# Graph layer on one NeuronCore: slot fill on the SyncE queue, node roots and residuals on GpSimd, a quarter of the node rows on VectorE

## The chip, the cores and the metric

One Trainium2 chip, one of its NeuronCores. The metric is the device time of one execution in microseconds (us). Times before: 1316.05, 1317.16 and 1323.12 us, median 1317.16.

## The reference

100,000 nodes with 160 features (64 scalars, 32 vectors of 3) and 25,000 edges sorted by `dst`. Cut to what matters:

```python
h = relu(layernorm(x))                          # per node, eps 1e-5
w = relu(edge_feature @ W_fc1) @ W_fc2          # 224 weights per edge
xs, xv = (s @ W_nl0)[dst], (v @ W_nl1)[dst]     # s, v: scalar and vector part of h
tp  = products of w, xs, xv and the edge's unit vector          # per edge, 480 values
agg = segment_sum(tp, src, N) / 32              # summed into the src node
out_s = agg_s @ W_out_s + s @ W_skip0
out_v = agg_v @ W_out_v + v @ W_skip1
x = x + [silu(out_s[:, :64]), sigmoid(out_s[:, 64:96]) * out_v]
```

## The kernel before

It is written engine by engine: each engine runs its own list of instructions in order, and semaphores tie them together. There are three stages.

**Opening.** Edges lie in 200 tiles of 125. A rank loop of 200 steps counts, for each edge, how many edges before it go to the same group of nodes: PE adds one-hots up (`count`, L1283), VectorE reads the result off (`tensor_tensor_reduce`, L648) and makes the next one-hot (L575). From the ranks VectorE makes `sidx` (L758), the row of the table `slots` in DRAM to which each edge's message goes. Meanwhile the table is filled with blank rows: 14 DMAs of 2744 KB each, issued by ScalarE (L1135). SyncE issues 20 small weight loads (L390) and the first edge features (L400). ScalarE, once its fills are issued, writes padding into the message ring `msg` (L1138), takes the square root for the unit vectors (L1141) and, when the weights are in, scales `fwd` (L1143). At step 30 of the rank loop PE multiplies `mirror` by `fwd` (L1346) and waits for that scaling. GpSimd gathers rows of x for the edges by indirect DMA (L495), `FIRST_GATHERS` = 132 tiles ahead of anything else.

**Edge stage.** 50 groups of 4 tiles. Per round PE makes the weights, rows and messages of a group, VectorE the products and the gathered rows' normalisation. On GpSimd four scatters (L505) write a finished group's messages to their slots, followed by as many gathers as the rule `due` (L526) asks for. GpSimd waits for the fill, for `sidx` and for the message (`e_fix`).

**Node stage.** 98 macro tiles of 1024 nodes (128 partitions, G = 8 rows each), in rounds. All engines go through `macros` (L341): 8 rounds written out, loops of 8, the rest written out. In round i:
- SyncE stores tile i-1 (`store_o`, L420) after its residual, loads the slots of tile i+3 (`load_m`) and x of tile i+7 (`load_x`, L407) into the place of the ring `xb` (8 places) that tile i-1 leaves.
- VectorE does `gate` (L984) for the two halves of a tile, `residual` (L998, adds x to the output), `hot_n` (L972, one-hots of the slots' local places), `stats_n` (L898, mean and variance of the rows of tile i+6). In one round of four (`u % U == 2`) it also turns the statistics of the next four tiles into n_rstd and n_bias: `spread`, `squares`, `variance`, `halve`, `seed`, three Newton steps, `shift_n` (L911 to L970). `n.ln` tells ScalarE.
- ScalarE normalises 8 rows of a tile, 4 in each half (`norm`, L1228), evacuates transposed rows with a relu (`evacuate`, L1237) and makes the gates' tanh and silu (L1242).
- PE transposes the normalised rows (`turn`), multiplies by the skip weights (`skip`), and adds the slots' messages (`add`).

GpSimd has nothing to do in the node stage.

## Time and profile before

| | |
|---|---|
| median of three runs | 1317.16 us |
| the profiled execution | 1322.71 us, its span 1320.8 us |
| PE, VectorE, ScalarE, GpSimd busy | 1114.8, 1026.3, 865.9, 442.2 us |
| opening | 0 to about 223 us |
| edge stage | to about 640 us |
| node stage | to the end |
| DMA moved | 271.10 MB |

The profile page gives an engine's busy time; what bounds a stage is read from the waits and from the chain of work that ended last. PE's busy time is modelled, since its matmuls overlap. Idle time counts only on the engine that the others wait for.

### The profile page before, as it was taken

How to read it: one execution, taken by the hardware profiler on the slowest of the kernel's cores; microseconds unless marked ns; L12 is line 12 of the kernel's file. 1: busy time of each engine (PE TensorE's matmuls, PEld its weight loads, DVE VectorE, ACT ScalarE, POOL GpSimd, SP SyncE). 2: the span in 40 equal slices, each digit the busy share in tenths (PEclk: the TensorE clock that was granted, in tenths of full speed). 3: DMA queues.
4: the chain of work that ended last, by engine and by line, in shares of the span. 5: the costliest groups of instructions: out<-in, count | busy, mean ns of one | idle time of the engine just before them, and what ended most of it. 6: DMA issues, size and time to landing. Idle time of an engine off the chain costs nothing.

```text
span 1320.8 us, 29100 instructions
## 1 busy us (share of the span) xinstructions
PE 1114.8 (84%) x8847; PEld 938.2 (71%) x8847; DVE 1026.3 (78%) x4002; ACT 865.9 (66%) x2070; POOL 442.2 (33%) x410
## 2 busy tenths in 40 slices
PE   5003998999999999989698999888998889988996
PEld 4002666888888888778577777777777777777775
DVE  8004998898888889776487888888888888888875
ACT  0003012787788778565677888788887888878884
POOL 6777710578787877777200000000000000000000
PEclk9556998999999999798699999999999999999998
DMA  9998200344544475444476677767777677666762
GB/s 358 406 406 308 66 23 9 91 132 133 130 130 135 129 244 176 122 114 123 128 256 241 246 265 255 252 230 262 257 259 259 222 264 256 250 252 239 261 213 108
DMA packets 108457, 271.10 MB, mean 205 GB/s; under 512 B 13573, under 2 KB 51751, under 8 KB 108364
## 3 DMA queue, kind: packets, MB, share of 16 engines
q1 hardware_dynamic: 76396, 194.15, 42.7%
q0 software_dynamic: 19200, 36.48, 9.4%
q10 hardware_dynamic: 12768, 39.34, 7.5%
q8 instruction: 45, 0.74, 0.2%
q14 instruction: 48, 0.39, 0.1%
HBM read 126.91 MB, written 143.01 MB: 204 GB/s over the span
## 4 chain that ended last, share of the span: by engine, by line
PE 35%; DVE 20%; issue 13%; POOL 13%; ACTq 8%; ACT 6%; DMA 2%; DVEq 0%; SPq 0%; POOLq 0%
POOL slots L505 9%; PE bank L1452 9%; ACTq L1135 8%; DVE n_stat L903 5%; DVE ob L994 4%; POOL xg L495 4%; PE bank L1465 4%; ACT nn L1233 4%; PE bank L1444 4%; PE bank L1284 3%; PE bank L1381 3%; PE bank L1456 2%; PE bank L1410 2%; DMA xb<-x 2%; PE bank L1316 2%
## 5 line engine op out<-in xcount | busy, mean ns | idle before, releaser
L1233 ACT ACTIVATE nn<-xb,n_bias,n_rstd 128x160 f32<-128x160 f32 x784 | 346.0, 526 | 87.8 <-DVE n_bias L634 87.8
L505 POOL DMA_INDIRECT slots<-msg,sidx x200 | 230.3, 1152 | 135.6 <-DVE sidx L758 71.4
L903 DVE BATCH_NORM_STATS2 n_stat<-xb 128x6 f32<-128x160 f32 x784 | 203.1, 314 | 11.9 <-DMA xb<-x 11.6
L994 DVE SCALAR_TENSOR_TENSOR ob<-sg,bank 128x128 f32<-128x128 f32 x588 | 132.7, 281 | 97.0 <-ACT ob L1248 95.8
L1452 PE MATMUL bank<-fwd,nt 128*128 128x160 f32 x784 | 146.5, 310 | 67.0 <-DVE ob L994 66.1
L1465 PE MATMUL bank<-mg,hot 64*128 64x192 f32 x1568 | 173.3, 340 | 9.2 <-DVE hot L979 9.2
L1452 PEld LDWEIGHTS bank<-fwd,nt 128*128 128x128 f32 x784 | 113.0, 191 | 81.4 <-issue 61.1
L495 POOL DMA_INDIRECT xg<-x,dst_i x136 | 148.6, 1093 | 44.1 <-issue 38.6
L1240 ACT ACTIVATE nt<-bank 128x640 f32<-128x640 f32 x196 | 137.2, 700 | 22.3 <-PE bank L1445 18.2
L1444 PE MATMUL bank<-ident,nn 128*128 128x128 f32 x784 | 147.0, 311 | 2.6 <-ACT nn L1233 2.6
L1001 DVE TENSOR_TENSOR ob<-ob,xb 128x1280 f32<-128x1280 f32 x98 | 146.0, 1490 | 2.6
L1444 PEld LDWEIGHTS bank<-ident,nn 128*128 128x128 f32 x784 | 109.1, 207 | 47.3 <-issue 46.2
L648 DVE CUSTOM_DVE_ANT_0 rank_junk<-bin_hot,bank 125x196 bf16<-125x196 f16 x200 | 70.6, 353 | 91.8 <-PE bank L1284 91.8
L1452 PE MATMUL bank<-rev,nt 128*128 128x160 f32 x784 | 140.3, 302 | 0.0
L1465 PEld LDWEIGHTS bank<-mg,hot 64*128 64x128 f32 x1568 | 125.6, 190 | 9.4 <-DVE hot L979 9.4
L1452 PEld LDWEIGHTS bank<-rev,nt 128*128 128x128 f32 x784 | 118.8, 193 | 0.0
L1189 ACT ACTIVATE tpt<-bank 128x375 f32<-128x375 f32 x200 | 96.6, 483 | 33.6 <-PE bank L1381 33.3
L1381 PE MATMUL bank<-ident,tp 125*128 125x125 f32 x600 | 107.7, 290 | 8.0 <-DVE tp L829 7.4
L1381 PEld LDWEIGHTS bank<-ident,tp 125*128 125x128 f32 x600 | 70.9, 150 | 43.3 <-issue 28.8
L1456 PE MATMUL bank<-fwd,nt 64*128 64x64 f32 x392 | 85.5, 299 | 0.0
L1456 PE MATMUL bank<-rev,nt 64*128 64x64 f32 x392 | 85.5, 298 | 0.0
L979 DVE TENSOR_TENSOR hot<-iota_local,mg 128x256 f32<-128x256 f32 x196 | 75.9, 419 | 11.5 <-DMA mg<-slots 11.5
(181 smaller groups left out, 2399.7 us busy)
## 6 DMA issues: line engine op xcount, KB each, us to landing
xb<-x SPq DMA_DIRECT2D x97, 640.0 KB, 5.1
out_dram<-ob SPq DMA_DIRECT2D x97, 640.0 KB, 3.3
slots<-blank ACTq DMA_DIRECT2D x14, 2744.0 KB
mg<-slots SPq DMA_DIRECT2D x98, 392.0 KB, 4.0
messages<-msg SPq DMA_DIRECT2D x50, 382.8 KB
ef<-edge_feat_t SPq DMA_DIRECT2D x50, 125.0 KB
slots<-msg,sidx POOLq DMA_INDIRECT x200, 4.3
xg<-x,dst_i POOLq DMA_INDIRECT x136, 6.8
```

The costliest lines, as they stand in the source:

```text
L495: pool.indirect_dma_start(rows_of(g)[:, t, :], None, x[:, :], bass.IndirectOffsetOnAxis(ap=dst_i[:, m:m + 1], axis=0)).then_inc(e_x[g % XS ...
L505: pool.indirect_dma_start(slots[:, :], bass.IndirectOffsetOnAxis(ap=sidx[:, m:m + 1], axis=0), msg[:, c, t, 0:MW], None).then_inc(e_sc[c], 16)
L903: done = dve.bn_stats(n_stat[:, u // U, u % U * G + g, :], xb[:, u, g, :])
L994: last = dve.scalar_tensor_tensor(out=o[:, :, S + V * j:S + V * j + V], in0=sg[:, h, :, :], scalar=1.0, in1=z[:, :, part], op0=ALU.add, op ...
L1001: dve.tensor_tensor(o, o, xb[:, u, :, :], ALU.add).then_inc(n.res, 1)
L1233: last = act.activation(nn[:, u % 2, h, spread_of(g % 4)], xb[:, u, g, order_of(g % 4)], ACT.Relu, bias=n_bias[:, u // U, c:c + 1], scale= ...
L1240: act.activation(nt[:, h, :], q_t[h], ACT.Relu).then_inc(n.ht, 1)
L1381: last = pe.transpose(p_tt[:, i * ET:(i + 1) * ET], tp[:, c, t, TURN[i]:TURN[i] + P], idt)
L1444: pe.transpose(q_t[h][:, t * P:(t + 1) * P], nn[:, u % 2, h, main_of(t)], ident[:])
L1452: pe.matmul(z[:, t, 0:F], nt[:, h, t * P:(t + 1) * P], sides[t // 2][:, skip_cols], start=(t % 2 == 0), stop=False, skip_group_check=True)
L1456: pe.matmul(z[:, 2 * j:2 * j + 2, F:Z], nt[part, h, 4 * P:5 * P], sides[j][part, skip_z_cols], start=False, stop=every, skip_group_check=True)
L1465: last = pe.matmul(q_z[h][:, t, 0:Z], hot[slots, u % 2, pair, :], mg[slots, u % U, pair, 0:Z], start=False, stop=True, skip_group_check=True)
```

## The change

**Opening.** The 14 fills go to SyncE, behind its first four edge loads; the weight loads go to ScalarE, ahead of all else there; the square root comes before the padding. VectorE blanks `blank` after the weight tiles. PE multiplies `mirror` by `fwd` at step 60 instead of 30. `FIRST_GATHERS` is 104 instead of 132, and `due` is smaller.

```diff
-    FIRST_GATHERS = 132
+    FIRST_GATHERS = 104
...
-                sp.wait_ge(s_clr, 1)
-                for to, of in weight_loads:
-                    sp.dma_start(to, of).then_inc(s_w, 16)
...
                 for q in range(ER):
                     load_f(q)
+                sp.wait_ge(s_blank, 2)
+                for k in range(NM // FILL):
+                    rows = slots[k * (FILL * BPM * P):(k + 1) * (FILL * BPM * P), :]
+                    sp.dma_start(rows.rearrange("(b p k) c -> p b (k c)", p=P, k=BPM),
+                                 blank[:, 0:BPM * MW].unsqueeze(1).to_broadcast((P, FILL, BPM * MW))).then_inc(s_fill, 16)
...
-                    due = min(NT, max(FIRST_GATHERS + 3 * (p + 1) // 2, GE * (p + 12)))
+                    due = min(NT, max(FIRST_GATHERS + 2 * (p + 1), GE * (p + 10)))
...
             def _(act):
+                act.wait_ge(s_clr, 1)
+                for to, of in weight_loads:
+                    act.dma_start(to, of).then_inc(s_w, 16)
+                act.wait_ge(s_tab, 1)
+                act.activation(vec_r[:], vec_d2[:], ACT.Sqrt).then_inc(s_sqrt, 1)
                 act.wait_ge(s_blank, 2)
-                for k in range(NM // FILL):
...
-                    if t == 30:
+                    if t == 60:
                         pe.wait_ge(s_fwd, 1)
```

**Node stage.** From tile 4 on GpSimd makes the roots with a power of -0.5, per tile (`root`), from sums that it makes for four tiles at once (`spread`); it also does the residual. VectorE keeps the root work of tiles 0 to 3. VectorE normalises row 3 of each half by a multiply-add without the relu, which `evacuate` applies anyway; ScalarE does the other three. PE's transposes wait for both. The statistics of a tile are made in two halves, before and after a gate. ScalarE and VectorE now wait for the shifts of one tile, not of four.

```diff
+                def nodes(n):
+                    def spread(j, w):
...
+                        pool.wait_ge(n.stats, min(j + U, NM) if isinstance(j, int) else j + U)
+                        pool.tensor_tensor(sums[:, 0, :], stat[:, :, 1], stat[:, :, 4], ALU.subtract)
+                        pool.tensor_tensor(sums[:, 1, :], stat[:, :, 2], stat[:, :, 5], ALU.add).then_inc(n.chain, 1)
+                        pool.tensor_tensor(sums[:, 2, :], stat[:, :, 1], stat[:, :, 4], ALU.add).then_inc(n.spread, U)
+                        pool.wait_ge(n.chain, base + 1)
+                        pool.tensor_tensor(sums[:, 3, :], sums[:, 0, :], sums[:, 0, :], ALU.mult)
+                        pool.tensor_scalar(sums[:, 1, :], sums[:, 1, :], 1.0 / F, EPS, ALU.mult, ALU.add).then_inc(n.chain, 1)
+                        pool.wait_ge(n.chain, base + 2)
...
+                        pool.tensor_scalar(sums[:, 3, :], sums[:, 3, :], 0.25, None, ALU.mult).then_inc(n.chain, 1)
+                        pool.wait_ge(n.chain, base + 3)
+                        pool.tensor_tensor(sums[:, 4, :], sums[:, 3, :], sums[:, 1, :], ALU.add).then_inc(n.chain, 1)
+                    def root(v, w):
...
+                        pool.tensor_tensor(n_rstd[:, b, cols], n_sum[:, b, 4, cols], neg_half[:], ALU.pow
+                                           ).then_inc(n.chain, 1)
+                        pool.tensor_scalar(n_sum[:, b, 2, cols], n_sum[:, b, 2, cols], -0.5, None, ALU.mult
+                                           ).then_inc(n.half, 1)
+                        pool.wait_ge(n.chain, base + 5 + k)
+                        pool.wait_ge(n.half, v - U + 1)
+                        pool.tensor_tensor(n_bias[:, b, cols], n_sum[:, b, 2, cols], n_rstd[:, b, cols], ALU.mult
+                                           ).then_inc(n.ln, 1)
+                    def residual(i, u):
+                        pool.wait_ge(n.mul, 2 * i + 2)
+                        o = ob[:, u % U, :, :]
+                        pool.tensor_tensor(o, o, xb[:, u, :, :], ALU.add).then_inc(n.res, 1)
+                    def round_n(i, u):
+                        v, w = i + 2, (u + 2) % XU
+                        if macro_exists(v) and macro_exists(i - 2):
+                            if w % U == 0:
+                                spread(v, w)
+                            root(v, w)
+                        if macro_exists(i - 1):
+                            residual(i - 1, (u + 7) % XU)
...
+                    def norm(i, u, h):
+                        dve.wait_ge(n.ln, i + 1)
+                        wait(dve, n.t, 2 * (i - 2) + h + 1)
+                        g = 4 * h + 3
+                        c = u % U * G + g
+                        dve.tensor_scalar(nn[:, u % 2, h, spread_of(3)], xb[:, u, g, order_of(3)],
+                                          n_rstd[:, u // U, c:c + 1], n_bias[:, u // U, c:c + 1],
+                                          ALU.mult, ALU.add).then_inc(n.norm_d, 1)
...
                         if macro_exists(i - 1):
                             gate(i - 1, before, 1)
...
+                        if macro_exists(i + 1):
+                            norm(i + 1, after, 1)
                         if macro_exists(i + 1) and not every:
                             hot_n(i + 1, after, 0)
                             hot_n(i + 1, after, 1)
...
+                        if measure:
+                            stats_n(s, v, 0, 4)
                         gate(i, u, 0)
...
+                        if macro_exists(i + 2):
+                            norm(i + 2, (u + 2) % XU, 0)
+                        if measure:
+                            stats_n(s, v, 4, 8)
...
-                        for g in range(4 * h, 4 * h + 4):
+                        for g in range(4 * h, 4 * h + 3):
...
                         pe.wait_ge(n.norm, 2 * i + h + 1)
+                        pe.wait_ge(n.norm_d, 2 * i + h + 1)
```

VectorE in two node rounds without root work, before (gates in banks 2 and 3 are the halves 0 and 1 of a tile):

```order
L994 SCALAR_TENSOR_TENSOR ob<-sg,bank3 128x4x32 x3
L1001 TENSOR_TENSOR ob<-ob,xb 128x1280
L979 TENSOR_TENSOR hot<-iota_local,mg 128x256 x2
L903 BN_STATS n_stat<-xb 128x6 x8
L994 SCALAR_TENSOR_TENSOR ob<-sg,bank2 128x4x32 x3
L994 SCALAR_TENSOR_TENSOR ob<-sg,bank3 128x4x32 x3
```

And now, in every round:

```order
L1066 SCALAR_TENSOR_TENSOR ob<-sg,bank3 128x4x32 x3
L1052 TENSOR_SCALAR nn<-xb,n_rstd,n_bias 128x160
L1042 TENSOR_TENSOR hot<-iota_local,mg 128x256 x2
L966 BN_STATS n_stat<-xb 128x6 x4
L1066 SCALAR_TENSOR_TENSOR ob<-sg,bank2 128x4x32 x3
L1052 TENSOR_SCALAR nn<-xb,n_rstd,n_bias 128x160
L966 BN_STATS n_stat<-xb 128x6 x4
```

The residual over 1280 columns is gone from VectorE, two multiply-adds over 160 columns have come, and the second half of the statistics stands behind a gate.

GpSimd, which had nothing behind its last scatter, now, from there on: a residual, the spread and root of tile 4, then a root and a residual for each tile (a spread every fourth):

```order
L513 DMA slots<-msg,sidx 50776x196 x36
L575 TENSOR_TENSOR ob<-ob,xb 128x1280
L545 TENSOR_TENSOR n_sum<-n_stat 128x32
L546 TENSOR_TENSOR n_sum<-n_stat 128x32
L547 TENSOR_TENSOR n_sum<-n_stat 128x32
L549 TENSOR_TENSOR n_sum<-n_sum 128x32
L550 TENSOR_SCALAR n_sum<-n_sum 128x32
L553 TENSOR_SCALAR n_sum<-n_sum 128x32
L555 TENSOR_TENSOR n_sum<-n_sum 128x32
L563 TENSOR_TENSOR n_rstd<-n_sum,neg_half 128x8
L565 TENSOR_SCALAR n_sum<-n_sum 128x8
L569 TENSOR_TENSOR n_bias<-n_sum,n_rstd 128x8
```

All node work of GpSimd stands behind its 200 scatters. Behind the spread and root comes the next residual (L575).

SyncE at the start of the program, now; the fills stand where the weight loads were, one place later:

```order
L394 DMA vec<-edge_vec 125x600
L403 DMA ef<-edge_feat_t 128x250 x4
L411 DMA slots<-blank 128x7x784 x14
L403 DMA ef<-edge_feat_t 128x250 x4
L398 DMA messages<-msg 125x4x196
```

The first edge loads have moved ahead of the fills, and the loads for round 4 and after stand behind all 14 of them.

## Rows read from the trace of the kernel before

**Rows 1.** The page's first line.
```profile
span 1320.8 us, 29100 instructions
```

**Rows 2.** The waits of the whole span: engine, line, released by, total us, times, longest.
```profile
ACT L1138 <- issue: 106.2, 1, 106.2
...
PE bank L1346 <- ACT fwd L1143: 89.0, 1, 89.0
ACT nn L1233 <- DVE n_bias L634: 87.8, 24, 4.2
POOL slots L505 <- DVE sidx L758: 71.4, 1, 71.4
PE bank L1452 <- DVE ob L994: 66.1, 47, 2.0
...
DVE n_stat L903 <- DMA xb<-x: 11.6, 24, 1.0
```

**Rows 3.** Timeline of GpSimd: start us, us, instruction, idle before and its releaser.
```profile
170.97 0.97 POOL L495 DMA_INDIRECT xb<-x,dst_i  x1 [0.30 <-issue]
243.29 1.00 POOL L505 DMA_INDIRECT slots<-msg,sidx  x1 [71.36 <-DVE sidx L758]
...
302.62 1.93 POOL L505 DMA_INDIRECT slots<-msg,sidx  x1 [0.30 <-issue]
...
638.87 0.97 POOL L505 DMA_INDIRECT slots<-msg,sidx  x1 [0.30 <-issue]
```

**Rows 4.** Busy us by stretch: PE, PEld, DVE, ACT, POOL; clock, DMA share, GB/s.
```profile
250.00:300.00 50.00, 50.00 (x413) 43.89 (x412) 45.82 (x174) 39.40 (x88) 39.99 (x33) 1.00 0.49 132
...
800.00:900.00 100.00, 88.36 (x729) 74.60 (x729) 84.87 (x319) 80.29 (x205) 0.00 (x0) 1.00 0.70 250
```

**Rows 5.** Groups of GpSimd, 260 to 500 us: busy us, mean ns, idle before.
```profile
L505 POOL DMA_INDIRECT slots<-msg,sidx x115 | 142.2, 1236 | 35.0 <-issue 31.7 <-DVE msg L845 3.4
L495 POOL DMA_INDIRECT xg<-x,dst_i x43 | 51.3, 1193 | 13.1 <-issue 11.0 <-DVE msg L845 2.1
```

**Rows 6.** The chain that ended last, in order of time, node stage.
```profile
777.74 1.32 PE bank L1452 x8
...
1240.42 1.32 PE bank L1452 x8
```

**Rows 7.** Timeline of SyncE's queue, first and last weight loads of 20.
```profile
3.34 4.82 SPq L390 DMA_DIRECT2D wfc<-W_fc  x4
...
31.15 1.53 SPq L390 DMA_DIRECT2D fwd<-W_nl  x1
```

**Rows 8.** DMA queues, 38 to 42 us: packets, MB, share (q1 is SyncE's).
```profile
q1 hardware_dynamic: 285, 0.26, 19.0%
```

**Rows 9.** Timeline of ScalarE, the scaling of `fwd`.
```profile
115.86 0.29 ACT L1143 ACTIVATE fwd<-fwd 128x128 f32<-128x128 f32 x1
```

**Rows 10.** Timeline of VectorE, one operation of two scalars over 200 columns.
```profile
4.50 0.27 DVE L565 TENSOR_SCALAR hi<-src_i 125x200 int32<-125x200 int32 x1 [0.66 <-DMA dst_i<-dst]
```

**Rows 11.** Timeline of VectorE and of SyncE's queue in a node round.
```profile
912.74 0.68 DVE L994 SCALAR_TENSOR_TENSOR ob<-sg,bank 128x128 f32<-128x128 f32 x3
...
916.56 1.49 DVE L1001 TENSOR_TENSOR ob<-ob,xb 128x1280 f32<-128x1280 f32 x1
...
919.40 0.80 SPq L409 DMA_DIRECT2D xb<-x  x1
...
924.50 1.91 DVE L903 BATCH_NORM_STATS2 n_stat<-xb 128x6 f32<-128x160 f32 x8 [0.45 <-DMA xb<-x]
```

**Rows 12.** Groups of GpSimd, 0 to 180 us: its work other than DMA.
```profile
L511 POOL TENSOR_SCALAR_AFFINE_SELECT ident<-ident 128x128 f32<-128x128 f32 x1 | 0.4, 410 | 0.0
...
L513 POOL TENSOR_SCALAR_AFFINE_SELECT mirror<-mirror 128x128 f32<-128x128 f32 x1 | 0.3, 282 | 0.0
...
L1543 POOL MEMSET const-float32-0.0<- 128x1 f32 x1 | 0.1, 98 | 0.3 <-issue 0.3
```

**Rows 13.** Timeline of VectorE, a product with both inputs in SBUF, edge stage.
```profile
302.61 0.42 DVE L823 TENSOR_TENSOR cr_b<-w4xv,hat 125x256 f32<-125x256 f32 x1
```

More of the change, by code:

```diff
@@ L254, in __init__ @@
                 self.root = sem(f"{name}_root")
+                self.stats = sem(f"{name}_stats")
+                self.spread = sem(f"{name}_spread")
+                self.chain = sem(f"{name}_chain")
+                self.half = sem(f"{name}_half")
+                self.norm_d = sem(f"{name}_norm_d")
                 self.ln = sem(f"{name}_ln")
@@ L529, in _ @@
                     made = max(made, due)
+                def nodes(n):
+                    def spread(j, w):
+                        b, base = w // U, 2 * (j - U)
+                        stat, sums = n_stat[:, b, :, :], n_sum[:, b, :, :]
+                        pool.wait_ge(n.stats, min(j + U, NM) if isinstance(j, int) else j + U)
[6 more added lines that the diff above has]
+                        pool.wait_ge(n.chain, base + 2)
+                        pool.sem_inc(s_held, 1)
+                        pool.tensor_scalar(sums[:, 3, :], sums[:, 3, :], 0.25, None, ALU.mult).then_inc(n.chain, 1)
+                        pool.wait_ge(n.chain, base + 3)
+                        pool.tensor_tensor(sums[:, 4, :], sums[:, 3, :], sums[:, 1, :], ALU.add).then_inc(n.chain, 1)
+                    def root(v, w):
+                        k, b = w % U, w // U
+                        base, cols = 2 * (v - k - U), slice(w % U * G, w % U * G + G)
+                        pool.wait_ge(n.chain, base + 4 + k)
+                        wait(pool, n.norm, 2 * (v - XU) + 2)
+                        wait(pool, n.norm_d, 2 * (v - XU) + 2)
+                        pool.tensor_tensor(n_rstd[:, b, cols], n_sum[:, b, 4, cols], neg_half[:], ALU.pow
[18 more added lines that the diff above has]
+                            residual(i - 1, (u + 7) % XU)
+                    macros(pool, round_n)
+                    residual(NM - 1, (NM - 1) % XU)
@@ L531, in _ @@
+                pool.wait_ge(s_half, 1)
+                nodes(main)
                 pool.wait_ge(b_fin, 1)
@@ L901, in stats_n @@
                             dve.wait_ge(n.x[u], earlier(i, u, XU, 16) + 16)
+                            if u % U == 0:
+                                wait(dve, n.spread, i - XU)
                         for g in range(first, last):
                             done = dve.bn_stats(n_stat[:, u // U, u % U * G + g, :], xb[:, u, g, :])
-                        if last == G and (u % U == U - 1 or isinstance(i, int) and i == NM - 1):
-                            done.then_inc(n.root, 1)
+                        if last == G:
+                            done.then_inc(n.stats, 1)
                     def level(i, u):
@@ L914, in spread @@
                         stat, sums = n_stat[:, b, :, :], n_sum[:, b, :, :]
-                        dve.wait_ge(n.root, base + 1)
+                        dve.wait_ge(n.stats, U)
                         dve.tensor_tensor(sums[:, 0, :], stat[:, :, 1], stat[:, :, 4], ALU.subtract)
@@ L922, in squares @@
                         sums = n_sum[:, b, :, :]
-                        dve.wait_ge(n.root, base + 2)
+                        dve.wait_ge(n.root, base + 1)
                         dve.tensor_tensor(sums[:, 3, :], sums[:, 0, :], sums[:, 0, :], ALU.mult)
@@ L936, in halve @@
                         b, base = u // U, level(i, u)
-                        dve.wait_ge(n.root, base + 4)
+                        dve.wait_ge(n.root, base + 3)
                         dve.tensor_scalar(n_seed[:, b, :], n_sum[:, b, 4, :].bitcast(I32), 1, None,
@@ L943, in seed @@
                         wait(dve, n.norm, 2 * (i - U))
-                        dve.wait_ge(n.root, base + 5)
+                        dve.wait_ge(n.root, base + 4)
                         dve.tensor_scalar(n_rstd[:, b, :].bitcast(I32), n_seed[:, b, :], -1.0, SEED, ALU.mult,
@@ L950, in root_a @@
                         y = n_rstd[:, b, :]
-                        dve.wait_ge(n.root, base + 7)
+                        dve.wait_ge(n.root, base + 6)
                         dve.tensor_tensor(n_step[:, b, 0, :], y, y, ALU.mult).then_inc(n.root, 1)
@@ L962, in root_c @@
                         y = n_rstd[:, b, :]
-                        dve.wait_ge(n.root, base + 9)
+                        dve.wait_ge(n.root, base + 8)
                         dve.scalar_tensor_tensor(out=y, in0=n_step[:, b, 1, :], scalar=1.5, in1=y,
@@ L968, in shift_n @@
                         b, base = u // U, level(i, u)
-                        dve.wait_ge(n.root, base + 16)
+                        dve.wait_ge(n.root, base + 15)
                         shift(n_bias[:, b, :], n_sum[:, b, :, :], n_rstd[:, b, :]).then_inc(n.ln, U)
@@ L996, in gate @@
                         last.then_inc(n.mul, 1)
-                    def residual(i, u):
-                        dve.wait_ge(n.mul, 2 * i + 2)
-                        o = ob[:, u % U, :, :]
-                        dve.tensor_tensor(o, o, xb[:, u, :, :], ALU.add).then_inc(n.res, 1)
                     def places(i):
```

66 lines of the change are left out of this document (11 added, 55 removed).

## The prediction

> **What bounds the kernel now.** I read the page first, then the waits, then timelines of the three stages, then the chain. The span is 1320.8 us [rows 1].
>
> The opening. The waits [rows 2] name one cause under three heads: ScalarE's first activation waits 106.2 us for its own queue, which is issuing the 14 fills of the slot table; PE waits 89.0 us at step 30 of the rank loop for `fwd`, which ScalarE scales only after that, and VectorE waits with it; GpSimd waits 71.4 us for `sidx`, which the rank loop ends in. GpSimd's last opening gather starts at 170.97, its first scatter at 243.29 [rows 3].
>
> The edge stage. From 250 on PE is 50.00 busy of 50 [rows 4], but GpSimd is full too: between 260 and 500 its 115 scatters and 43 gathers take 193.5 us of issue and 48.1 us of gaps [rows 5], the whole 240 us, and only 5.5 us of the gaps wait for a message of VectorE. So it is behind the other engines, and its last scatter, begun at 638.87 [rows 3], opens the node stage. That is 396.5 us for 268 indirect DMAs, 1.48 us each.
>
> The node stage. The chain passes the same instruction every fourth macro tile at 777.74 and, 17 such steps on, at 1240.42 [rows 6]: 27.2 us for four, 6.8 for one. PE is busy 88.36 of 100 us [rows 4], so without waits four would take about 24.0. The rest are waits around the one round in four in which VectorE also does the root: PE for the gate 66.1 us, ScalarE for the shifts 87.8 us; loads of `xb` cost VectorE only 11.6 us [rows 2].
>
> **Part 1, fill and loads change queues.** ScalarE now issues the 20 weight loads first. On SyncE they went out from 3.34 to 32.7, 1.5 us each beside the same fill [rows 7]. By 38 to 42 that queue moves packets of 0.9 KB, edge rows that were queued behind the weights [rows 8], so the weights are through by then. What stands between the queue's end and `fwd` on ScalarE, the square root and the padding of `msg`, takes 115.9 - 106.2 = 10 us [rows 9, 2], so `fwd` is ready near 43. PE asks for it at step 60. It stood at step 30 at 116 - 89 = 27 us, which bounds 30 steps from above, and the 170 steps after the wait run until the `sidx` of rows 3 at 243, so at least 0.5 us each: step 60 falls between 42 and 54, and the wait is gone or a few us. I leave 3 us for that and for slower steps beside GpSimd's gathers. On SyncE only four edge loads stand ahead of the fill, and the next thing behind it is an edge load for round 4, after the fill is out; the fill's issue ended at 106 us [rows 2] and shifts by a few us, so it stays well ahead of the first scatter. Rank loop and first scatter move by 89 - 3 = 86 us, to 157.
>
> GpSimd does not get all of that. It issues 104 gathers first instead of 132, at 1.25 us (0.95 and a gap of 0.30 [rows 5, 3]): done at 172 - 35 = 137, idle for 20. Then 296 indirect DMAs are left, 28 more than before. At 1.48 us they take 438 us: last scatter at 595 instead of 640. **Gain 45 us.** The mean between 260 and 500, 1.52 us, would give 607 and 33 us; all 86 us would come only if GpSimd were no limit, which its full issue contradicts, but its DMAs are quicker when PE and VectorE stall. I keep 25 to 60.
>
> **Part 2, node rounds.** ScalarE loses two of eight activations of 526 ns a round; VectorE loses the residual of 1.49 us and all root work and gains two multiply-adds over 160 columns, 0.24 us each (200 columns took 0.27 [rows 10]). The waits for shifts go: roots are now made by GpSimd ahead of time. What is late next is the load of `xb`. SyncE may load x(i+7) only after the residual of tile i-1, which frees the buffer, and VectorE's statistics of x(i+7) come two rounds later than that residual. One residual ends at 918.05, its x load, the third on the queue, is issued at 919.40, and the statistics that need it start at 924.50 after a wait [rows 11]: 6.45 us. Only 0.45 us of it is waited for now. A longer residual lengthens exactly this ring.
>
> The new ring over two rounds: 6.45 for the load; half the statistics 0.90 (half of 1.91); gate 0.60 (0.68, the next begins 0.60 after its start); multiply-add 0.20; second half 0.95: 9.1. Then either the gate of the other half and a handover, 0.85, and the residual r; or, once in four rounds, GpSimd's spread and root s, which wait for those statistics and stand ahead of the residual on its queue, and then r. Four rounds: 2 x 9.1 + 0.85 + 2r + s = 19.05 + 2r + s.
>
> The trace shows no such work on GpSimd. For r the nearest row is its own masked copy of 128 columns, 282 ns [rows 12]: ten times that, 2.8 us, which I take. Ends: VectorE's 1.49 us for the same residual, and the slower copy, 410 ns, times ten, 4.1 us. For s, ten small instructions and five waits on itself: taken 0.28 x 10 + 5 x 0.15 = 3.5; ends 1.0 (ten of its 98 ns fills, no handover) and 4.1 + 1.5 = 5.6 (the slow copy, gaps of 0.30). Sum 19.05 + 5.6 + 3.5 = 28.2 against 27.2. **Loss** 1.0 x 24.5 = **25 us**, with ends of 24.0 (PE's floor), a gain of 78, and 32.9, a loss of 140. If the ring is as computed, VectorE's and ScalarE's relief is worth nothing.
>
> Edits that cost nothing: the start of the residual on GpSimd in the last tile (1.3 us, in the rounding), the -0.5 fill, the extra semaphores.
>
> **Sum.** The profiled execution took 1322.7 us with its launch: 1322.7 - 45 + 25 = 1302.7. It lay 5.5 us above the median of the three runs, 1317.2, so I give 1298.
>
> **Rivals.**
> (a) GpSimd and VectorE stop each other. In the edge stage a scatter takes 1.93 us instead of 0.97 when it falls into VectorE's back-to-back products (302.61 and 302.62 [rows 13, 3]), while those products keep their 0.42 us, as long as the 256-column one-hots of the node stage. If each residual loses that 1.0 us to the two one-hots and the multiply-add that VectorE sends right behind the gate that releases it, r is 3.8, four rounds take 30.2, and the loss is 3.0 x 24.5 = 74 us: 1317 - 45 + 74 = 1346, slower. It decides from r = 3.2 on, where the whole gain of 45 is eaten up. For it: the order of VectorE's round. Against: here they are three instructions of 0.9 us in all, against a run of eight there. By the Trainium skill ("SBUF — State Buffer", Who interferes with whom), a VectorE instruction with two SBUF inputs and a GpSimd one that reads SBUF exclude each other for a whole instruction, whichever starts first. By that rule VectorE's one-hots could wait out a whole residual, too, but they stand ahead of a wait for the x load that is as long, so only the residual's own delay counts; the stretched scatter agrees with a lock, the unchanged products do not show it in the other direction.
> (b) GpSimd adds nearly as fast as VectorE: r = 1.5 to 2.0, s = 2.5, four rounds in 24.6 to 25.6, a gain of 40 to 64: 1208 to 1232. For it: if 98 of the copy's 282 ns are a fixed start, as in the one-column fill, ten times the rest and one start make 1.9 us. Against: the copy reads one input, the residual two. By the Trainium skill ("GPSIMD Engine Reference", Performance versus the Vector engine) a two-input add there takes 1.96 times VectorE's time; an estimate by it is 2.9 us for this residual, and 1304 where the sum has 1298.
> (c) The weights land only with the fill, so that `fwd` waits for 112 us as before and the rank loop still stands from step 60: first scatter at 224, 296 DMAs then end at 662, 22 us later than now: 1317 + 22 + 25 = 1364. Rows 8 speak against it.
> (d) The change does not do what it says, because GpSimd reaches the node work late: it comes after the last scatter on its queue. Node rounds cannot start before that scatter anyway.
>
> **Chances.** Forecast (both parts as computed, r near 2.8) 0.52; (a) 0.19; (b) 0.19; (c) 0.05; the rest, in both directions, 0.05. The forecast's own range, from a gain of 25 to 60 us in part 1 and r within 0.4 of 2.8 (20 us), is 1263 to 1338. For 8 in 10 I reach over most of (a) and into (b): 1230 to 1352, which leaves out the better half of (b), (c) and the top of (a). A measurement here can tell about 0.5%, 6.6 us, from no change. Faster by more: three quarters of the forecast, (b) and 0.02 of the rest, 0.60. Within: an eighth of the forecast and the mild fifth of (a), 0.11. Slower: what is left of these, (c) and 0.03 of the rest, 0.29.
>
> **What would show it.** Right: PE's wait at the mirror matmul gone; first scatter near 157 after a GpSimd idle time near 20; last scatter near 595; in the node stage, VectorE waiting for `xb<-x` by 1 to 3 us in most rounds, chain through GpSimd's residual and that load, four tiles in 28. Wrong: residuals under 2 us, or x loads not waited for; a first scatter after 200; VectorE's one-hots stretched past 1 us with nothing waiting for x.

## The result, and the profile after

| | before | after |
|---|---|---|
| time, median | 1319.8 us (4 runs, 1316.1 to 1323.1) | 1352.0 us (4 runs, 1347.5 to 1356.7) |
| profiled execution: time, span | 1322.7, 1320.8 us [rows 1] | 1348.3, 1346.5 us |
| after / before | | 1.0245, 95% interval 1.0189 to 1.0301 |
| four macro tiles, node stage | 27.2 us [rows 6] | 30.7 us |

The change makes the kernel 2.5% slower; 1298 us was predicted, faster. One execution of run 5 below took 2505 us, nearly twice its other three, and stands in none of its figures. Line numbers of the kernel after are its own: the residual on GpSimd is L575, the power L563, VectorE's multiply-add L1052, its one-hots L1042, its gate L1066, its statistics L966.

**The opening went as computed.** GpSimd's timeline, to be held against [rows 3]:

```profile
137.45 1.04 POOL L503 DMA_INDIRECT xb<-x,dst_i  x1 [0.30 <-issue]
148.80 1.01 POOL L513 DMA_INDIRECT slots<-msg,sidx  x1 [10.31 <-DVE sidx L819]
...
586.44 0.97 POOL L513 DMA_INDIRECT slots<-msg,sidx  x1 [0.30 <-issue]
```

The first scatter starts at 148.8 after 10.3 us of idle time (predicted: 157 and 20), the last at 586.4 instead of 638.9 (predicted: 595). So the node stage starts 52 us earlier, and all of that and 32 us more is lost later. The wait at the mirror matmul is gone: ScalarE scales `fwd` at 37.11.

```profile
37.11 0.31 ACT L1174 ACTIVATE fwd<-fwd 128x128 f32<-128x128 f32 x1
```

**The node stage waits for x.** The waits of the whole span, against [rows 2]:

```profile
DVE n_stat L966 <- DMA xb<-x: 173.5, 74, 5.4
...
POOL ob L575 <- DVE ob L1066: 96.3, 49, 14.0
PE bank L1484 <- DVE ob L1066: 94.1, 52, 4.7
POOL n_sum L545 <- DVE n_stat L966: 75.8, 22, 4.0
...
ACT nn L1264 <- POOL n_bias L569: 56.0, 43, 1.7
...
DVE ob L1066 <- ACT ob L1279: 41.8, 39, 2.9
```

VectorE's wait for the loads of x grew from 11.6 to 173.5 us, while ScalarE's for the shifts fell from 87.8 to 56.0. The windows (columns as in [rows 4]) show that no engine is full in this stage, and that PE's granted clock, 1.00 there before, is 0.89:

```profile
800.00:900.00 100.00, 83.83 (x623) 70.45 (x621) 71.48 (x233) 62.46 (x153) 74.15 (x74) 0.89 0.64 228
```

**The ring, row by row.** The ring is the circle residual, load of x into the place that it frees, statistics of that x, gate, next residual. One period of four tiles in the timelines of GpSimd, VectorE and SyncE's queue:

```profile
917.74 2.91 POOL L575 TENSOR_TENSOR ob<-ob,xb 128x1280 f32<-128x1280 f32 x1
...
922.01 0.76 SPq L417 DMA_DIRECT2D xb<-x  x1
...
927.09 1.00 DVE L966 BATCH_NORM_STATS2 n_stat<-xb 128x6 f32<-128x160 f32 x4 [3.90 <-DMA xb<-x]
...
929.78 0.66 DVE L1066 SCALAR_TENSOR_TENSOR ob<-sg,bank 128x128 f32<-128x128 f32 x3
...
930.52 3.63 POOL L575 TENSOR_TENSOR ob<-ob,xb 128x1280 f32<-128x1280 f32 x1 [1.96 <-DVE ob L1066]
...
935.52 0.77 SPq L417 DMA_DIRECT2D xb<-x  x1
...
940.94 1.01 DVE L966 BATCH_NORM_STATS2 n_stat<-xb 128x6 f32<-128x160 f32 x4 [0.22 <-DMA xb<-x]
...
943.80 0.29 POOL L545 TENSOR_TENSOR n_sum<-n_stat 128x32 f32<-128x32 f32 x1 [3.69 <-DVE n_stat L966]
...
946.01 1.67 POOL L563 TENSOR_TENSOR n_rstd<-n_sum,neg_half 128x8 f32<-128x8 f32 x1
...
948.14 2.91 POOL L575 TENSOR_TENSOR ob<-ob,xb 128x1280 f32<-128x1280 f32 x1
```

Read downwards, each row starts when the one above it lets it: a residual of 2.91; 6.44 us until the statistics of the x that it lets in; 3.43 through statistics, gate, multiply-add and second gate to the next residual; that residual, 3.63; 6.79 to the next statistics; 2.86 to the spread; spread and root 4.34, of which the power alone is 1.67; and the residual again. The sum is 30.40 us. Over nine such periods the mean is 30.70, by the residuals ahead of the spread, in GpSimd's timeline:

```profile
906.91 2.96 POOL L575 TENSOR_TENSOR ob<-ob,xb 128x1280 f32<-128x1280 f32 x1 [1.50 <-DVE ob L1066]
...
1183.21 2.96 POOL L575 TENSOR_TENSOR ob<-ob,xb 128x1280 f32<-128x1280 f32 x1 [1.73 <-DVE ob L1066]
```

This is the ring that the prediction described, and it closes; its terms were too small. In the period shown no step of the ring waits for PE or ScalarE. The ring is read from the waits: the profile's own chain stays on GpSimd's queue here and passes no load of x between 626 and 1259 us.

**Each engine holds the other up.** The groups of VectorE and GpSimd in the whole span (busy us, mean ns of one):

```profile
L1042 DVE TENSOR_TENSOR hot<-iota_local,mg 128x256 f32<-128x256 f32 x196 | 134.8, 727 | 10.6 <-DMA mg<-slots 10.6
L1052 DVE TENSOR_SCALAR nn<-xb,n_rstd,n_bias 128x160 f32<-128x160 f32 x196 | 125.5, 641 | 0.8 <-POOL n_bias L569 0.4
...
L575 POOL TENSOR_TENSOR ob<-ob,xb 128x1280 f32<-128x1280 f32 x98 | 303.9, 3101 | 96.3 <-DVE ob L1066 96.3
L563 POOL TENSOR_TENSOR n_rstd<-n_sum,neg_half 128x8 f32<-128x8 f32 x94 | 156.6, 1666 | 3.3 <-POOL n_sum L555 2.2
```

The one-hots took 419 ns each before, as the groups of that kernel have it:

```profile
L979 DVE TENSOR_TENSOR hot<-iota_local,mg 128x256 f32<-128x256 f32 x196 | 75.9, 419 | 11.5 <-DMA mg<-slots 11.5
```

The means of the one-hots and the multiply-adds after hide two kinds each, as VectorE's timeline shows beside two residuals (906.91 to 909.87, and 930.52 to 934.15 above):

```profile
907.02 3.47 DVE L1042 TENSOR_TENSOR hot<-iota_local,mg 128x256 f32<-128x256 f32 x2
...
917.95 2.79 DVE L1052 TENSOR_SCALAR nn<-xb,n_rstd,n_bias 128x160 f32<-128x160 f32 x1
...
930.63 0.75 DVE L1042 TENSOR_TENSOR hot<-iota_local,mg 128x256 f32<-128x256 f32 x2
```

At 907.02 the pair of one-hots ends only after the residual; at 930.63 it takes its usual 0.75 us and the residual 3.63 instead of 2.91. The multiply-add of 917.95, 0.36 us elsewhere, lasts until the residual of 917.74 ends.

### The profile page after: what moved, and what is told of

Its sections match the earlier page's. It is cut to its first block, busy times and chain, and to the rows that moved or that the text cites. A ratio compares the mean times of both kernels' runs of the same rounds, so it can differ in the third digit from the quotient of the medians.

```text
span 1346.5 us, 29745 instructions
## 1 busy us (share of the span) xinstructions
PE 1158.7 (86%) x8847; PEld 972.3 (72%) x8847; DVE 1001.3 (74%) x3669; ACT 805.8 (60%) x1873; POOL 1005.6 (75%) x958
## 4 chain that ended last, share of the span: by engine, by line
issue 32%; POOL 29%; PE 26%; DVE 7%; DMA 3%; POOLq 1%; SPq 0%; ACT 0%; DVEq 0%
POOL n_rstd L563 9%; POOL ob L575 6%; POOL slots L513 6%; POOL xg L503 4%; PE bank L1412 4%; PE bank L1315 3%; PE bank L1441 3%; PE bank L1347 2%; PE bank L1429 2%; DVE bin_hot L636 2%; PE bank L1425 2%; PE bank L1484 2%; PE bank L1427 2%; DMA xb<-x 2%; DVE rank_junk L709 2%
## 5 line engine op out<-in xcount | busy, mean ns | idle before, releaser
L575 POOL TENSOR_TENSOR ob<-ob,xb 128x1280 f32<-128x1280 f32 x98 | 303.9, 3101 | 96.3 <-DVE ob L1066 96.3
L966 DVE BATCH_NORM_STATS2 n_stat<-xb 128x6 f32<-128x160 f32 x784 | 196.0, 311 | 173.5 <-DMA xb<-x 173.5
L1264 ACT ACTIVATE nn<-xb,n_bias,n_rstd 128x160 f32<-128x160 f32 x588 | 264.0, 521 | 56.2 <-POOL n_bias L569 56.0
L1484 PE MATMUL bank<-fwd,nt 128*128 128x160 f32 x784 | 156.6, 325 | 94.7 <-DVE ob L1066 94.1
L1484 PEld LDWEIGHTS bank<-fwd,nt 128*128 128x128 f32 x784 | 122.5, 205 | 111.5 <-issue 70.0
L1497 PE MATMUL bank<-mg,hot 64*128 64x192 f32 x1568 | 185.7, 359 | 10.9 <-DVE hot L1042 10.9
L1476 PE MATMUL bank<-ident,nn 128*128 128x128 f32 x784 | 153.4, 321 | 10.4 <-DVE nn L1052 9.8
L1066 DVE SCALAR_TENSOR_TENSOR ob<-sg,bank 128x128 f32<-128x128 f32 x588 | 130.9, 277 | 41.9 <-ACT ob L1279 41.8
L563 POOL TENSOR_TENSOR n_rstd<-n_sum,neg_half 128x8 f32<-128x8 f32 x94 | 156.6, 1666 | 3.3 <-POOL n_sum L555 2.2
L1278 ACT ACTIVATE sg<-bank 128x128 f32<-128x128 f32 x196 | 53.0, 271 | 172.5 <-PE bank L1497 145.6
L1497 PEld LDWEIGHTS bank<-mg,hot 64*128 64x128 f32 x1568 | 135.0, 202 | 11.0 <-DVE hot L1042 11.0
L1042 DVE TENSOR_TENSOR hot<-iota_local,mg 128x256 f32<-128x256 f32 x196 | 134.8, 727 | 10.6 <-DMA mg<-slots 10.6
L1052 DVE TENSOR_SCALAR nn<-xb,n_rstd,n_bias 128x160 f32<-128x160 f32 x196 | 125.5, 641 | 0.8 <-POOL n_bias L569 0.4
## 6 DMA issues: line engine op xcount, KB each, us to landing
slots<-blank SPq DMA_DIRECT2D x14, 2744.0 KB, 30.7
```

The source lines that it names most:

```text
L563: pool.tensor_tensor(n_rstd[:, b, cols], n_sum[:, b, 4, cols], neg_half[:], ALU.pow).then_inc(n.chain, 1)
L575: pool.tensor_tensor(o, o, xb[:, u, :, :], ALU.add).then_inc(n.res, 1)
L966: done = dve.bn_stats(n_stat[:, u // U, u % U * G + g, :], xb[:, u, g, :])
L1042: made = dve.tensor_tensor(hot[:, u % 2, bins, :], iota_local[:].unsqueeze(1).to_broadcast((P, 2, P)), mg[:, m, bins, LOCAL:LOCAL + 1].to_ ...
L1264: last = act.activation(nn[:, u % 2, h, spread_of(g % 4)], xb[:, u, g, order_of(g % 4)], ACT.Relu, bias=n_bias[:, u // U, c:c + 1], scale= ...
L1476: pe.transpose(q_t[h][:, t * P:(t + 1) * P], nn[:, u % 2, h, main_of(t)], ident[:])
```

## The experiments

Two theories stood against each other. **Ring theory**: the load of x waits for the residual, so whatever GpSimd does between the statistics and the end of the residual lengthens the node stage. **Lock theory**: GpSimd's residual and VectorE's one-hots and multiply-adds stop each other, and that is what costs. Each run has 4 executions (run 3 has 10), the kernel before 7 or 13 on the same chip (medians 1321.1, 1320.2 and 1323.2 us in the order of the three groups: 1 to 4, 5 to 8, 9 to 12). Ratios are to that kernel; differences to the change are to its 1352.0 us, and a few us between runs of different groups say nothing.

### 1. The opening alone

The kernel before with the first half of the change: fill on SyncE, weights on ScalarE, fewer gathers ahead. Its moves of fill and weights are those of the change; the rest of its edit:

```diff
-    FIRST_GATHERS = 132
+    FIRST_GATHERS = 104
...
-                    due = min(NT, max(FIRST_GATHERS + 3 * (p + 1) // 2, GE * (p + 12)))
+                    due = min(NT, max(FIRST_GATHERS + 2 * (p + 1), GE * (p + 10)))
...
-                    if t == 30:
+                    if t == 60:
```

> The kernel before with the opening of the change alone (fill on SyncE, weight loads on ScalarE, step 60, 104 first gathers), its node stage as before. If the two parts add up, this keeps what the profile of after shows for the opening, a last scatter at 586 instead of 639 us, and loses nothing in the node stage at 27.2 us for four tiles: about 1320 - 52 = 1267 us. If the opening's gain were given back in the node stage by other means (the fill's queue, the clock), it would stay above 1300.

Measured 1272.9 us, ratio 0.9646 (0.961 to 0.968). Part 1 gains 48 us by itself, so part 2 loses 79 from there, not 25.

### 2. The residual back on VectorE

The first line stood in GpSimd's round, the second comes in VectorE's.

```diff
-                            residual(i - 1, (u + 7) % XU)
...
                             gate(i - 1, before, 1)
+                            residual(i - 1, before)
```

> The changed kernel with the residual back on VectorE, right behind the gate that ends a tile; roots stay on GpSimd, one row in four on VectorE. Ring theory (the load of x waits for the residual; residual, power and spread on GpSimd make the ring long): the ring has neither a GpSimd residual nor the roots in it, 6.45 + 3.25 + 1.5 = 11.2 us for two tiles, so PE's 24 to 25 us for four sets the pace: 1352 - 6 x 24.5 = about 1205 to 1215 us. Lock theory (GpSimd's two-input work stops VectorE's two-input and one-source work wherever they meet): the power of 1.67 us still stops VectorE once a tile, now also its residual, VectorE has 5.6 + up to 1.7 us of work a tile: 27 to 29 us for four, 1260 to 1310 us.

Measured 1227.1 us, ratio 0.9289 (0.925 to 0.933): 125 us less than the change, 12 us above the ring theory's figure and 33 us below the lock theory's. VectorE's wait for the loads of x falls from 173.5 to 4.5 us, and PE is busy 95 of 100 us at a clock of 1.00, as that kernel's windows show:

```profile
900.00:1000.00 100.00, 95.25 (x790) 80.85 (x787) 91.48 (x300) 76.24 (x190) 47.35 (x77) 1.00 0.75 269
```

### 3 and 4. A root without the power; the one-hots ahead of the gate

In run 3 the root is a product: the roots themselves are left out, so the normalised values are others. In run 4 VectorE's multiply-add and one-hots come ahead of the gate that releases the residual.

```diff
-                        pool.tensor_tensor(n_rstd[:, b, cols], n_sum[:, b, 4, cols], neg_half[:], ALU.pow
+                        pool.tensor_tensor(n_rstd[:, b, cols], n_sum[:, b, 4, cols], neg_half[:], ALU.mult
```

> The changed kernel with a product in place of the power of -0.5 on GpSimd, so the roots are left out and the rows are scaled wrongly; the work is otherwise the same. A product over 8 columns should take 0.2 us instead of 1.67. Ring theory: the ring holds the power once in four tiles, so four tiles take 1.45 us less: 1352 - 36 = 1316 us. If GpSimd's total time were the bound (its busy share is 75%), all four powers would count: 1352 - 142 = 1210. If neither, no change.

Measured 1325.4 us, ratio 1.0043 (1.001 to 1.008): 27 us less than the change, 9 us short of what the ring theory gave. The product in its groups:

```profile
L563 POOL TENSOR_TENSOR n_rstd<-n_sum,neg_half 128x8 f32<-128x8 f32 x94 | 19.1, 203 | 3.3 <-POOL n_sum L555 2.2
```

It took 203 ns against 1666, and 1.46 us once in four tiles is 36 us; GpSimd was not full (56 to 60 of 100 us busy between 700 and 1200 us). The residuals, 3280 ns in the mean, were held longer than in the change, which can be the 9 us; that is not shown. The power stands in the ring.

```diff
-                        if macro_exists(i - 1):
-                            gate(i - 1, before, 1)
                         if macro_exists(i + 1):
                             norm(i + 1, after, 1)
...
+                        if macro_exists(i - 1):
+                            gate(i - 1, before, 1)
```

> The changed kernel with VectorE's multiply-add and one-hots of a round moved ahead of the gate that releases GpSimd's residual; nothing else. Lock theory: they no longer run into the residual, so one-hots fall from a mean of 0.73 us to 0.42 and the multiply-add from 0.64 to under 0.5; what the measured 30.7 us for four tiles has above the ring's 29.3 goes: 1.4 x 24.5 = 34 us, about 1318 us. Ring theory without a lock: these instructions stand in the wait for x anyway, 1345 to 1355 us.

Measured 1363.1 us, ratio 1.0318 (1.027 to 1.037). The lock theory expected a gain and missed; the ring theory's 1345 to 1355 was 8 us too low. Groups of that kernel:

```profile
L1042 DVE TENSOR_TENSOR hot<-iota_local,mg 128x256 f32<-128x256 f32 x196 | 74.0, 418 | 20.6 <-DMA mg<-slots 10.6 <-PE bank L1497 9.7
...
L575 POOL TENSOR_TENSOR ob<-ob,xb 128x1280 f32<-128x1280 f32 x98 | 284.9, 2907 | 123.8 <-DVE ob L1066 123.8
```

The one-hots are down to 418 ns, the residuals to 2.91 us each, and still it takes 11 us longer: the 61 us of one-hot time that were saved had been spent where VectorE then waited for x anyway (those waits grow from 173.5 to 242.5 us), and the two instructions now stand in the ring, ahead of the gate: from statistics to residual 4.38 us (906.49 to 910.87 in that kernel's timeline), against 3.43. The multiply-adds of the other half round stayed held (635 ns), so this run does not speak about them.

### 5 and 6. All normalising on ScalarE

```diff
-                        for g in range(4 * h, 4 * h + 3):
+                        for g in range(4 * h, 4 * h + 4):
```

VectorE's `norm` and its waits go. Run 5 does this to the change, run 6 to run 2, so that only the roots and shifts of part 2 stay on GpSimd.

> The change, with all four rows of a half tile normalised on ScalarE again; the two multiply-adds of VectorE per tile are gone, the residual and the roots stay on GpSimd. In the change these multiply-adds take 641 ns each in the mean (125.5 us for 196) and as little as 349 ns where nothing stretches them: 57 us are stretch, and each stretched one stands ahead of the second half of the statistics, whose buffer had landed. Ring theory alone (no stop between the engines): the ring loses two multiply-adds of 0.36 us in four tiles, 0.72 x 24.5 = 18 us, to about 1334. Lock theory (GpSimd's residual holds the multiply-add up, and that delay lies in the ring): the 57 us go as well, to about 1277. Either way ScalarE gets 0.9 us more a tile, 62 of 100 us busy now, some 76 then, which should not bind.

Measured 1347.9 us, ratio 1.0239 (1.017 to 1.031): 4 us less than the change, which is no difference, so both theories missed. Its lines of the waits show where the 57 us of held multiply-adds may have gone:

```profile
DVE n_stat L965 <- DMA xb<-x: 227.2, 68, 6.9
...
DVE ob L1065 <- ACT ob L1271: 86.3, 73, 3.2
```

VectorE's waits for ScalarE, whose fourth row stands ahead of the activations that the gate needs, doubled to 86.3 us, and those for x grew by 54. That the fourth row is the cause was not tested.

> The change with the residual and all normalising where they were before (VectorE right behind the gate; ScalarE), so that of part 2 only the roots and shifts are GpSimd's. Against the run with the residual on VectorE and one row of four on VectorE (1227.1 us), it tells what the multiply-add is worth: VectorE is 91.5 of 100 us busy there and PE 95. Either theory: if VectorE's load is what is left, 0.7 us a tile less for it gives 0 to 20 us, 1207 to 1227; if ScalarE, which waits 64.9 us for shifts there and would get 0.9 us a tile more, becomes the late one, 1235 to 1255. Against the opening alone (1272.9 us) it tells what moving only the roots gives.

Measured 1211.6 us, ratio 0.9173 (0.914 to 0.921). Beside VectorE's own residual the multiply-adds cost 15 us. Run 6 against run 1 is the worth of moving the roots: 61 us, together with the halved statistics and the waits for the shifts of one tile, which run 6 keeps.

### 7. The load of x first

The wait for the residual moves out of `store_o` to the head of SyncE's round.

```diff
                         if macro_exists(i - 1):
-                            store_o(i - 1, (u + 7) % XU)
-                        if macro_exists(i + U - 1) and not every:
-                            load_m(i + U - 1, (u + U - 1) % XU)
+                            sp.wait_ge(n.res, i)
                         if isinstance(i, int) and i + 7 == NM - 1:
                             load_last((u + 7) % XU)
                         elif macro_exists(i + 7) and macro_exists(i - 1):
                             load_x(i + 7, (u + 7) % XU)
+                        if macro_exists(i - 1):
+                            store_o(i - 1, (u + 7) % XU)
+                        if macro_exists(i + U - 1) and not every:
+                            load_m(i + U - 1, (u + U - 1) % XU)
```

> The change, with SyncE's three DMAs of a round in another order: the load of x(i+7) first, then the store of tile i-1, then the slot rows. No engine's work changes. In the change the load is issued 1.36 us after the residual that frees its buffer ends, behind the store and the slot rows; here some 0.25. Ring theory: two such loads stand in the ring of four tiles, so it loses 2 x 1.1 = 2.2 us, 54 us in all, to about 1298. Lock theory (what costs is that GpSimd's residual and VectorE's one-hots and multiply-adds stop each other): nothing of that changes, 1345 to 1355.

Measured 1296.2 us, ratio 0.9828 (0.978 to 0.987), where the ring gave 1298. The load now leaves 0.19 us after its residual's end, as one period of that kernel's timeline has it:

```profile
892.43 2.90 POOL L577 TENSOR_TENSOR ob<-ob,xb 128x1280 f32<-128x1280 f32 x1
...
895.52 0.33 SPq L417 DMA_DIRECT2D xb<-x  x1
...
900.76 1.01 DVE L968 BATCH_NORM_STATS2 n_stat<-xb 128x6 f32<-128x160 f32 x4 [2.88 <-DMA xb<-x]
...
904.20 3.63 POOL L577 TENSOR_TENSOR ob<-ob,xb 128x1280 f32<-128x1280 f32 x1 [0.96 <-DVE ob L1068]
...
913.12 1.01 DVE L968 BATCH_NORM_STATS2 n_stat<-xb 128x6 f32<-128x160 f32 x4 [0.72 <-DMA xb<-x]
...
916.26 0.28 POOL L547 TENSOR_TENSOR n_sum<-n_stat 128x32 f32<-128x32 f32 x1 [1.10 <-DVE n_stat L968]
...
920.60 2.91 POOL L577 TENSOR_TENSOR ob<-ob,xb 128x1280 f32<-128x1280 f32 x1
```

The period is 28.17 us instead of 30.40. From a residual's end to the statistics it has 5.43 and 5.29 us instead of 6.44 and 6.79; the residuals, 2.90 and 3.63, and spread and root, 4.34, are as they were, the hold included. No engine's work changed, yet 56 us are gone. In the mean its residuals are held longer than in the change (3212 ns), its one-hots less (520 ns, 41 us in all); but run 4 freed the one-hots wholly and gained nothing. This run decides between the theories.

### 8. Eight more gathers first

```diff
-    FIRST_GATHERS = 104
+    FIRST_GATHERS = 112
```

> The run with the residual on VectorE (1227.1 us), with 112 instead of 104 gathers ahead of the first scatter. In the change GpSimd stands idle 10.3 us ahead of that scatter; eight more gathers of 1.25 us fill it, and the last scatter should come 8 to 10 us earlier: 1217 to 1219. If the first scatter comes later by as much, or gathers that follow wait for buffers, 1227.

Measured 1219.1 us, ratio 0.9221 (0.917 to 0.927): this is run 2 with that edit, and 8 us less than run 2.

### 9. The residual ahead of the root

```diff
+                        if macro_exists(i - 1):
+                            residual(i - 1, (u + 7) % XU)
                         if macro_exists(v) and macro_exists(i - 2):
                             if w % U == 0:
                                 spread(v, w)
                             root(v, w)
-                        if macro_exists(i - 1):
-                            residual(i - 1, (u + 7) % XU)
```

> The change, with GpSimd's round in another order: the residual of tile i-1 ahead of the spread and the root for tile i+2. The same work. In the change the residual that is queued behind the spread starts 4.0 us after its gate is through (gate through at 913.76, residual at 917.74). Ring theory, by the ring alone: 4.0 to 4.4 us of four tiles go, 98 to 108 us, to 1244 to 1254. If the shifts then become the late thing (spread and root end one residual of 2.9 us later, and ScalarE, which waits 1.7 us for them once in four tiles now, waits some 4.6): at most 2.9 of the 4.4 us come back, about 1315. Lock theory: VectorE's one-hots now meet a residual in every round, 1350 or more.

Measured 1443.1 us, ratio 1.0908 (1.087 to 1.095): both figures of the ring theory missed, and the lock theory's "1350 or more" covers it. VectorE waits no more for x (0.0 us), and another ring has closed, one round long. GpSimd, ScalarE and VectorE in that kernel's timeline:

```profile
907.73 2.96 POOL L575 TENSOR_TENSOR ob<-ob,xb 128x1280 f32<-128x1280 f32 x1 [2.67 <-DVE ob L1066]
...
910.66 1.84 POOL L563 TENSOR_TENSOR n_rstd<-n_sum,neg_half 128x8 f32<-128x8 f32 x1
...
913.11 1.35 ACT L1264 ACTIVATE nn<-xb,n_bias,n_rstd 128x160 f32<-128x160 f32 x3 [3.39 <-POOL n_bias L569]
...
914.51 0.36 ACT L1279 ACTIVATE ob<-bank 128x256 f32<-128x256 f32 x1
...
914.98 0.68 DVE L1066 SCALAR_TENSOR_TENSOR ob<-sg,bank 128x128 f32<-128x128 f32 x3 [0.60 <-ACT ob L1279]
...
915.74 2.95 POOL L575 TENSOR_TENSOR ob<-ob,xb 128x1280 f32<-128x1280 f32 x1 [2.67 <-DVE ob L1066]
```

The root waits behind the residual, ScalarE's normalising for the root, the activations for the gate behind that on ScalarE's queue, and the next residual for the gate: 8.01 us a round, and some 10.4 in the one with the spread. I had counted one late shift in four tiles; there is one in every tile. The one-hots are held in every round (1757 ns in the mean), but every row above is released by the one before it, and none of them is a held one; only the root is 0.17 us longer than in the change. Three rounds of 8.01 and one of 10.4 make 34.4 us for four tiles, 91 us more than the change over the node stage, which is what was measured.

### 10. Half the residual

Four of the eight row groups get no residual in this run.

```diff
-                        o = ob[:, u % U, :, :]
-                        pool.tensor_tensor(o, o, xb[:, u, :, :], ALU.add).then_inc(n.res, 1)
+                        o = ob[:, u % U, 0:G // 2, :]
+                        pool.tensor_tensor(o, o, xb[:, u, 0:G // 2, :], ALU.add).then_inc(n.res, 1)
```

> The change, with GpSimd's residual over four of the eight row groups only; the other half of the residual is left out. Ring theory: two residuals stand in the ring of four tiles, 2.91 and 3.63 us, and each loses half: 3.2 us, 78 us in all, to about 1274. If GpSimd's own time set the pace, all four would count: 4 x 1.45 = 5.8 us, which passes the best node stage measured so far, so about 1215. Lock theory without a ring: the holds of VectorE's one-hots (60 us in all over the unheld time) and multiply-adds (57 us) halve, 1290 to 1300.

Measured 1293.9 us, ratio 0.9814 (0.976 to 0.987). Four tiles take 28.4 us there (863.70 to 977.13 in four steps), and the pair of residuals in the ring 1.54 and 2.26 us: 2.74 us less than in the change, 67 us in all, of which 58 came; the ring theory, which expected the hold to halve too, gave 78. Two of four residuals set the pace, not GpSimd's whole time (1215); 1290 to 1300 was the lock theory's figure, so this run alone speaks for that one.

### 11 and 12. Towards the best version

Run 11 is run 6 with the edit of run 8, run 12 is run 11 with the edit of run 7.

> The version with only the roots and shifts on GpSimd (1211.6 us), with 112 gathers ahead of the first scatter. Eight more gathers took 8 us off the version with the residual on VectorE; if the two are independent, 1203 to 1205. If the edge stage's tail already hides it, 1211.

> The same with SyncE's load of x first in the round. With the residual on VectorE the loads of x cost VectorE only 27.1 us of waits, and PE is 97.5 of 100 us busy, so the ring no longer binds: 0 to 10 us, 1193 to 1204. If the later store of a tile holds up the gate that reuses its buffer: 1205 to 1215.

Measured 1207.0 us, ratio 0.912 (0.908 to 0.916), and 1206.3 us, 0.914 (0.909 to 0.919). Neither can be told from the other; run 11 is 8.8% faster than the kernel before. Where the ring does not bind, an earlier load gained nothing; that the later store took a gain back, the other expectation for run 12 (1205 to 1215), was not tested.

## Why the prediction was wrong

**What bounds the kernel, and part 1: right.** The fill and the weights were the cause of the wait for `fwd`, and GpSimd's queue kept about half of the rank loop's gain. The gain was sized at 45 us; alone it measured 48, and the last scatter moved by 52.

**Part 2: right ring, terms too small, and so the wrong sign.** The formula, 19.05 + 2r + s, gave 28.2 us for four tiles; the period shown above has 30.4. The step that failed is the sizing of r and s:

- s was taken as 3.5 (ten small instructions of 0.28 us and five handovers). It measured 4.34, because the ten are not alike: most take 0.20 to 0.30 us, and the power 1.67 on eight columns. That is 0.84 us, 21 us in all. Run 3 took the power out and got 27 us back.
- r was taken as 2.8 twice. One of the two is 2.91, near the estimate; the other is 3.63, held up by VectorE's one-hots (in run 4, where they come ahead of the gate, the mean is 2.91): 0.94 us together, 23 us in all.
- The rest of the ring, 19.05 by the prediction, measured 19.52 (6.44 + 3.43 + 6.79 + 2.86), 12 us in all: the second load landed 0.34 us later (VectorE's held one-hots were through 0.22 us before it), and the multiply-add takes 0.27 us until the next instruction starts, not 0.20.

By these terms the loss is 3.2 x 24.5 = 78 us, and 1317 - 45 + 78 = 1350 us, where 1352 was measured. Both r and s lay within the ends that the prediction had given (1.49 to 4.1 and 1.0 to 5.6); the middle of s was taken from copies and fills, and no row of the kernel before has a power. The forecast also stood closer to the point of no gain than it said: a loss of 1.8 us for four tiles eats 45 us, which with r at 2.8 needs s = 4.4 only. Rival (a) named such a point for r alone.

**"VectorE's and ScalarE's relief is worth nothing"**: right for the change as a whole (run 5 gives ScalarE its rows back, and the time stays), and it hid that its parts pull in opposite directions. By runs 1, 6 and 2 and the change, added in this order: opening -48, roots to GpSimd -61, one row in four to VectorE +15, residual to GpSimd +125. In another order the parts are others: with the residual on GpSimd the row in four costs nothing (run 5).

**Rival (a)** came closest in time (1346 us) but by another path. Holds in both directions are there, as it said, yet r was to lose 1.0 us in every round, and loses 0.7 in one residual of the two that count; that is 18 of the 79 us. Its row from the edge stage was not as plain as it read: the scatter before it, begun at 301.34 in the same products, took 0.98 us. By the Trainium skill ("SBUF — State Buffer", Who interferes with whom) a VectorE instruction with two SBUF inputs and a GpSimd one that reads SBUF exclude each other for a whole instruction. The trace agrees: 0.42 us became up to 3.15 for a one-hot. Its statement that the order of issue decides who blocks is not shown here by when records begin: the residual's record begins 0.11 us ahead of the one-hots both at 907.02, where they are held, and at 930.63, where it is. By the Trainium skill ("GPSIMD Engine Reference", Performance versus the Vector engine) a residual would be an estimated 2.9 us; it measured 2.91 where nothing held it, and that rule would have put the forecast up by 6 us, not to the other side.

**Rivals (b), (c) and (d)** fell: no residual under 2.8 us, `fwd` scaled at 37, and GpSimd, ready for the node work, waiting 14.0 us for VectorE's gate after its last scatter.

**What the prediction named as signs** came out in part: VectorE waits for x, 2.3 us at a time (173.5 in 74), and its waits lead through the residual and the x load, but the profile's own chain does not. The number that would have warned, four tiles in 30.7 instead of 28, is the whole error.

What stays open: PE's clock fell to 0.89 in the stretch that had 1.00 before. Runs 1 and 2 have 1.00 there, run 3 0.90 to 0.93 at a PE share (88 to 89) like run 1's. Run 7 has 0.97 to 1.00. The steps of the ring in the change and in run 7 add up without a wait for PE, so these periods need no share of the clock; no run changes the clock alone.

## To carry to other kernels

Before moving work off a busy engine, follow what its last instruction releases: here the residual frees a buffer whose reload, statistics and gate lead back to the next residual, and moving it cost 125 us, more than any relief elsewhere gave. Work that sits beside such a ring (the roots, with the residual on VectorE) is what to move, and an issue order that puts the reload ahead of the store and the other load takes 1.2 us off each load in the ring (run 7). Where a term of the sum is an operation that no row shows, work out at which value of it the sign turns, for each such term, and let that set the chance.

## What was not expected

A power on GpSimd costs 1.67 us for 128 x 8 values, a product of the same size 0.20 (run 3): eight times as much. The holds between GpSimd and VectorE are long but do not touch every instruction: beside residuals on GpSimd the statistics and gates kept their time, as run 5's timeline shows within one residual.

```profile
917.10 2.91 POOL L574 TENSOR_TENSOR ob<-ob,xb 128x1280 f32<-128x1280 f32 x1
...
917.60 1.00 DVE L965 BATCH_NORM_STATS2 n_stat<-xb 128x6 f32<-128x160 f32 x4
...
919.46 0.68 DVE L1065 SCALAR_TENSOR_TENSOR ob<-sg,bank 128x128 f32<-128x128 f32 x3 [0.86 <-ACT ob L1271]
```

And VectorE's residual holds GpSimd in turn: in run 2 a product of 32 columns, 0.24 us in the change, takes 1.50 beside it, while the residual takes 1.57 (1.51 in the mean).

```profile
918.73 1.57 DVE L1065 TENSOR_TENSOR ob<-ob,xb 128x1280 f32<-128x1280 f32 x1
918.91 1.50 POOL L549 TENSOR_TENSOR n_sum<-n_sum 128x32 f32<-128x32 f32 x1
```
